# An attention and expert kernel on one core: second sequence's norm ahead of the split, key parts stored once

## The reference, cut to what matters

```python
x = x + _L0_xattn_ref(_layernorm(x), ctx, ...)          # stage A
h = _layernorm(_layernorm(x), ln_w, ln_b)               # norms u, b
hc = conv(h, 3 taps per channel, causal)
q, k, v = split(hc @ attn_w)                            # 16 heads of 8
q = q * cos + _rotate_half(q) * sin;  k likewise
scores = einsum(q, k) / sqrt(8), causal
y = softmax(scores) @ v @ proj_w
...                                                     # experts
x = x + _L1_xattn_ref(_layernorm(x), ctx, ...)          # stage C: k, v = ctx @ Wkv, 16 heads of 64
x = x + _L1_ffn_ref(_layernorm(x), ...)
```

## Time and profile before

| what | value |
|---|---|
| median of 3 runs (lowest, highest) | 342.58 us (340.04, 346.72) |
| the profiled execution's own time | 340.81 us |
| its span in the trace | 338.6 us |
| mean granted TensorE clock | 0.993 |
| PE, PE weight loads, DVE, ACT, POOL busy, share of the span | 93%, 65%, 72%, 65%, 38% |
| of the chain that ended last: PE, DVE, ACT, DMA | 58%, 16%, 14%, 3% |

### The profile page before, as it was taken

One profiled execution on the slowest core, in us unless ns is written; L12 is line 12 of the kernel. 1 busy time (PEld: TensorE's weight loads), 2 busy tenths in 40 slices (PEclk: granted clock), 3 DMA queues, 4 the chain that ended last, 5 costly groups with the idle time before them and its releaser, 6 DMA issues.

```text
span 338.6 us, 6802 instructions
## 1 busy us (share of the span) xinstructions
PE 315.3 (93%) x2270; PEld 220.6 (65%) x2270; DVE 245.2 (72%) x758; ACT 220.0 (65%) x649; POOL 128.1 (38%) x183
## 2 busy tenths in 40 slices
PE   8799989998989999999989998998999999999886
PEld 3348778665554433345446998985778687878675
DVE  4988875784898988888811552479788877887576
ACT  1488885375365756756676765754676667686995
POOL 3455564110641444410640440410685434535400
PEclk9999999999999999999998999999999999999999
DMA  7590000076763430091001003100100000000002
GB/s 213 196 274 10 2 0 2 8 243 170 209 206 89 113 102 3 1 326 52 5 31 56 2 31 111 33 1 2 54 20 15 0 2 1 3 0 0 2 0 65
DMA packets 21881, 22.47 MB, mean 66 GB/s; under 512 B 3894, under 2 KB 18646, under 8 KB 21846
## 3 DMA queue, kind: packets, MB, share of 16 engines
q1 hardware_dynamic: 18982, 16.78, 17.4%
q10 hardware_dynamic: 2352, 4.20, 3.7%
q0 software_dynamic: 512, 1.05, 1.0%
HBM read 14.22 MB, written 7.60 MB: 64 GB/s over the span
## 4 chain that ended last, share of the span: by engine, by line
PE 58%; DVE 16%; ACT 14%; issue 5%; POOL 4%; DMA 3%; SPq 0%; ACTq 0%; POOLq 0%
PE PS L1388 51%; PE PS L1442 5%; DVE PS L872 5%; ACT big L1167 5%; ACT big L1364 3%; POOL big L529 2%; DVE big L690 2%; DVE big L715 2%; DMA big<-in_A_WkT 2%; ACT big L1305 1%; ACT big L1141 1%; DMA XN<-scr_y,pos 1%; DVE XN L667 1%; ACT cw L1141 1%; PE PS L1704 1%
## 5 line engine op out<-in xcount | busy, mean ns | idle before, releaser
L1388 PE MATMUL PS<-big 128*128 128x128 f32 (+10 forms) x592 | 93.3, 308 | 7.0 <-DVE big L690 2.1
L1388 PEld LDWEIGHTS PS<-big 128*128 128x128 f32 (+3 forms) x592 | 56.2, 150 | 39.7 <-DVE mB L872 18.2
L529 POOL TENSOR_TENSOR big<-big,urec 128x1024 f32<-128x1024 f32 x24 | 45.6, 1900 | 60.2 <-DVE urec L722 45.4
L1167 ACT ACTIVATE big<-big 128x154 f32<-128x154 f32 x192 | 60.5, 319 | 10.6 <-DVE big L690 5.6
L872 DVE CUSTOM_DVE_ANT_0 PS<-PS,later 128x128 f32<-128x128 f32 (+3 forms) x128 | 60.1, 517 | 8.9 <-PE PS L1388 7.7
L1305 ACT ACTIVATE big<-PS 128x1024 f32<-128x1024 f32 (+3 forms) x64 | 43.2, 701 | 25.0 <-PE PS L1388 25.0
L1141 ACT ACTIVATE big<-PS 128x1280 f32<-128x1280 f32 (+2 forms) x30 | 32.3, 1088 | 27.0 <-PE PS L1442 24.5
L1388 PE MATMUL PS<-kkC,XT 128*128 128x462 f32 (+1 forms) x96 | 36.0, 511 | 1.9 <-DVE big L715 1.9
L1167 ACT ACTIVATION_READ_ACCUMULATOR big<-big 128x1 f32 x192 | 36.2, 189 | 0.0
L517 POOL TENSOR_TENSOR rstd<-ve,minus_half 128x4 f32<-128x4 f32 (+2 forms) x13 | 13.2, 1017 | 56.3 <-DVE ve L662 56.3
L1388 PEld LDWEIGHTS PS<-vwCm,big 128*128 128x128 f32 x256 | 30.8, 192 | 3.9 <-ACT big L1141 1.3
(11 more groups left out here) (192 smaller groups left out, 499.7 us busy)
## 6 DMA issues: line engine op xcount, KB each, us to landing
scr_qk<-big SPq DMA_DIRECT2D x12, 384.0 KB, 3.3
big<-scr_qk SPq DMA_DIRECT2D x16, 288.0 KB
big<-in_wv ACTq DMA_DIRECT2D x1, 2048.0 KB, 7.9
scr_x<-zrow SPq DMA_DIRECT2D x2, 448.0 KB, 6.9
scr_y<-big SPq DMA_DIRECT2D x2, 448.0 KB, 3.4
X<-in_x ACTq DMA_DIRECT2D x2, 256.0 KB, 3.3
big<-in_A_WoT ACTq DMA_DIRECT2D x1, 512.0 KB, 4.7
cw<-in_C_Wk SPq DMA_DIRECT2D x1, 512.0 KB, 5.2
```

What stands on the lines that cost most here:

```text
L529: pool.tensor_tensor(pn[:, 0:GH * P].rearrange("p (h k) -> p h k", h=GH), Pt[u % 3][:, :, 0:KM], r.to_broadcast([P, GH, KM]), ALU.mult).th ...
L1167: i = act.activation(Pt[u % 3][:, h, :], Pt[u % 3][:, h, :], ACT.Exp, accum_out=usum[:, u % 3, h:h + 1])
L1388: return pe.matmul(o, lhsT, rhs, start=start, stop=stop)
```

## The change

For sequence 1, the statistics and the application of norm b move on DVE ahead of `split_first`, with `add_rotated` between them. `weigh_router` moves from ring step 1 to in front of `rotate(1)`. The table numbers move: sequence 1 is transposed after job 16 instead of 25, its query and key matmuls and its `xv` come after job 24 instead of 29, jobs 28 to 49 instead of 32 to 49 stand among the maxima (two each at steps 5 and 13), and the first maxima are turned after job 40 instead of 44. `values(0)` on ACT comes after the first maxima's copy, and sequence 0's ones and zeros in `vaug` are written by two memsets on POOL. Key parts are stored once in `scr_k` (24 rows), and each group of `ks` is loaded by three transfers of 24 rows.

```diff
-        scr_qk = nc.dram_tensor("scr_qk", (B, 2, SPLIT, HB, T), BF16, kind="Internal").ap()
+        scr_q = nc.dram_tensor("scr_q", (B, SPLIT, HB, T), BF16, kind="Internal").ap()
+        scr_k = nc.dram_tensor("scr_k", (B, SPLIT // 3, HB, T), BF16, kind="Internal").ap()
...
-        F_QKV = (14,30)
-        F_LN = 26
-        F_LATE = 32
-        F_VALUES = 42
-        F_MAX = 45
+        F_QKV = (14, 25)
+        F_LN = 17
+        F_LATE = 26
+        F_FIRST = 28
+        F_VALUES = 38
+        F_MAX = 41
+        M_TWICE = (5, 13)
...
-                    sp.dma_start(scr_qk[b, 1].rearrange("(x y d) h t -> y (d h) x t", x=3, y=3)[a],
-                                 P3[:, 1, a, :].unsqueeze(1).to_broadcast([P, 3, T])).then_inc(scr_written[b], 16)
+                    sp.dma_start(scr_k[b].rearrange("(y d) h t -> y (d h) t", y=3)[a], P3[:, 1, a, :]).then_inc(scr_written[b], 16)
...
-                    sp.dma_start(ks[b][0:SPLIT, hs, :], scr_qk[b, 1, :, hs, :]).then_inc(stack_ready[b][g], 16)
-                    sp.dma_start(qs[b][0:SPLIT, hs, :], scr_qk[b, 0, :, hs, :]).then_inc(stack_ready[b][g], 16)
+                    for x in range(3):
+                        sp.dma_start(ks[b][SPLIT // 3 * x:SPLIT // 3 * (x + 1), hs, :], scr_k[b, :, hs, :]).then_inc(stack_ready[b][g], 16)
+                    sp.dma_start(qs[b][0:SPLIT, hs, :], scr_q[b, :, hs, :]).then_inc(stack_ready[b][g], 16)
...
             pool.wait_ge(part_ready[1], 3)
+            pool.wait_ge(preC_act, sum(j[2] for j in PREC[:F_VALUES]))
+            v = vaug[:, 0].rearrange("p t h m -> p (t h) m")
+            pool.memset(v[:, :, HDB:HDB + 1], 1.0).then_inc(v_ready, 1)
+            pool.memset(v[:, :, HDB + 1:32], 0.0).then_inc(v_ready, 1)
             split_maxima(1)
...
             rotate(0)
+            ln_b_stats(1)
             add_rotated()
+            ln_apply("b", U, XN, 1)
             split_first()
-            ln_b_stats(1)
-            ln_apply("b", U, XN, 1)
             convolve(1)
+            weigh_router()
             rotate(1)
...
-            copy_C(F_LN, F_VALUES)
+            copy_C(F_LN, F_MAX)
+            copy_maxima(0)
             act.wait_ge(preC_act, sum(j[2] for j in PREC[:F_VALUES]))
             values(0)
-            no_values(0)
-            copy_C(F_VALUES, F_MAX)
-            copy_maxima(0)
...
-            fold_C(F_QKV[1], F_LATE)
-            pe.wait_ge(preC_act, sum(j[2] for j in PREC[:F_LATE]))
-            pe.wait_ge(qkv_read, 4 * B)
+            fold_C(F_QKV[1], F_FIRST)
+            pe.wait_ge(preC_act, sum(j[2] for j in PREC[:F_LATE - 2]))
...
-            late = F_LATE
+            late = F_FIRST
             for m in range(M0):
                 scores_for_maximum(m)
-                if m >= 2 and late < len(PREC):
+                for _ in range(2 if m in M_TWICE else 1):
                     fold_C(late, late + 1)
                     late += 1
-                if late == F_MAX:
-                    turn_maxima(0)
+                    if late == F_MAX:
+                        turn_maxima(0)
```

More of the change, by code:

```diff
@@ L470, in _ @@
                     sp.wait_ge(part_ready[b], a + 1)
-                    sp.dma_start(scr_qk[b, 1].rearrange("(x y d) h t -> y (d h) x t", x=3, y=3)[a],
-                                 P3[:, 1, a, :].unsqueeze(1).to_broadcast([P, 3, T])).then_inc(scr_written[b], 16)
-                    sp.dma_start(scr_qk[b, 0].rearrange("(x y d) h t -> x (d h) y t", x=3, y=3)[a],
+                    sp.dma_start(scr_k[b].rearrange("(y d) h t -> y (d h) t", y=3)[a], P3[:, 1, a, :]).then_inc(scr_written[b], 16)
+                    sp.dma_start(scr_q[b].rearrange("(x y d) h t -> x (d h) y t", x=3, y=3)[a],
                                  P3[:, 0, a, :].unsqueeze(1).to_broadcast([P, 3, T])).then_inc(scr_written[b], 16)
@@ L816, in ln_b_stats, with weigh_router @@
                 ln_stats("b", U, b, lambda: dve.wait_ge(ln_norm["u"], QT * b + QT))
+            def weigh_router():
+                dve.wait_ge(ld_b, 64)
+                dve.wait_ge(ld_vec, 16)
+                dve.wait_ge(zeroed, Z_ALL)
+                dve.tensor_scalar(rw2[:], rw[:], vec[:, V_LN2W:V_LN2W + 1], None, ALU.mult).then_inc(rw2_ready, 1)
+                dve.tensor_scalar(ln2b[:], ones[:], vec[:, V_LN2B:V_LN2B + 1], None, ALU.mult).then_inc(rw2_ready, 1)
             def convolve(b):
@@ L916, in x_plus_u @@
                 own.wait()
[L919 to L925, removed]
             def centre_router():
@@ L1023, in _ @@
                     normalise_group(*divmod(g, 4))
-                if s == 1:
-                    weigh_router()
-                elif s == 3:
+                if s == 3:
                     centre_router()
@@ L1238, in values @@
                 copy(v[:, :, 0:HDB], XN[:, QT * b:QT * b + QT, :].rearrange("p t (h d) -> p (t h) d", h=HB)).then_inc(v_ready, 1)
-                copy(v[:, :, HDB:HDB + 1], ones[:, 0:QT * HB].unsqueeze(2)).then_inc(v_ready, 1)
             def no_values(b):
                 v = vaug[:, b].rearrange("p t h m -> p (t h) m")
+                copy(v[:, :, HDB:HDB + 1], ones[:, 0:QT * HB].unsqueeze(2)).then_inc(v_ready, 1)
                 copy(v[:, :, HDB + 1:32], ones[:, 0:32 - HDB - 1].unsqueeze(1).to_broadcast([P, QT * HB, 32 - HDB - 1]),
@@ L1534, in fold_C @@
                         pe.wait_ge(ln_T["b"], B)
-                        pe.wait_ge(qkv_read, 4 * B)
+                        pe.wait_ge(qkv_read, 4 * B - 2)
                     elif 3 <= n < F_LATE:
@@ L1640, in scores_for_maximum @@
                 if m % M_CHUNK == 0:
-                    pe.wait_ge(stack_ready[0][m // M_CHUNK], 32)
+                    pe.wait_ge(stack_ready[0][m // M_CHUNK], 64)
                 if m >= 3:
                     pe.wait_ge(s_max, m - 2)
+                elif m == 1:
+                    pe.wait_ge(qkv_read, 4 * B)
+                elif m == 2:
+                    pe.wait_ge(preC_act, sum(j[2] for j in PREC[:F_LATE]))
                 for j in range(2):
@@ L1654, in ring_scores @@
                 if n % M_CHUNK == 0:
-                    pe.wait_ge(stack_ready[b][n // M_CHUNK], 32)
+                    pe.wait_ge(stack_ready[b][n // M_CHUNK], 64)
                 if k < 2:
@@ L1662, in ring_scores @@
                 i.then_inc(s1_mm, 1)
-            late = F_LATE
+            late = F_FIRST
             for m in range(M0):
                 scores_for_maximum(m)
-                if m >= 2 and late < len(PREC):
+                for _ in range(2 if m in M_TWICE else 1):
                     fold_C(late, late + 1)
                     late += 1
-                if late == F_MAX:
-                    turn_maxima(0)
+                    if late == F_MAX:
+                        turn_maxima(0)
+            assert late == len(PREC)
             def outputs(s):
```

1 line of the change is left out of this document (removed).

## The result

The changed kernel is slower: 345.88 us median of four runs (343.68 to 347.82) against 341.31 for the kernel before in the same rounds (339.29 to 346.72). The ratio is 1.0127, 95% interval 1.0084 to 1.0170; on a second chip it was 1.0088 (1.0046 to 1.0129). The forecast of 337.5 and its range miss it. The profiled execution took 343.68 us (span 341.8, mean clock 0.989) against 340.81 before (0.993). It is the fastest of the four; the others, 345.55 to 347.82, had a mean clock of 0.980 to 0.983 and left no trace, so what follows explains this one execution, and where the others lost more is not shown.

What follows compares the result with a forecast made beforehand. PE was 93% busy, with PE and DVE near bounds together in the maxima. Gains of 3.5 us by the maxima's end and 0.3 in the ring, 3.8, took 340.81 to 337.0; it chose 337.5, range 334.5 to 341.5.

Steps and rivals of the forecast that it cites:

- Norm b ahead of the split: Sequence 1 before its scores: convolution ends 3.8 us earlier, at 78.4; PE ready for scores at 84.6 instead of 87.83.
- The stacks: Key stores and loads ahead of the first scores: group 0 lands at 84.5, scores start at 84.7, a gain of 3.1.
- rival 1: Ahead of the first scores: group 0 lands at 86 to 87, start gains 1.3, time 339.3; chance 0.15.
- A late store delays PE directly: Ahead of the first scores: the loads' five us of cover are gone, so a late store holds up PE.
- The maxima: Stretch from first scores to last maximum: 19.6 us instead of 19.97, ending at 104.3 against 107.8.
- Three steps in flight let PE put folds into DVE's time: In the maxima: from step 0 on, the reason for taking 19.6 us, nearer to DVE's time.
- rival 2: In the maxima: four added folds cost their full 2.3, PE bounds the stage at 21.5 us, time 339.4; chance 0.15.
- The hole of 1.15: DVE's wait at 102.47 in the maxima, behind ACT's values, ones and zeros: goes away, 1.0 us counted as gained.
- the fourfold price: POOL's memsets of ones and zeros: 1.35 us by columns, free up to four times that, since POOL idled 5.35 us.
- The router: At the ring's start: `weigh_router` moved from step 1 to in front of `rotate(1)` gains 0.3 of 0.6 us.
- The DMA rule: Stack loads: 72 rows and 24 rows both run on 12 of 16 engines, so the keys' rate does not change.
- Rivals 4 and 5: Slower by SP's queue of load issues, about 345.5, or by transfers in series, 342.5; chance 0.04 each.

Runs made afterwards that it cites:

- keys thrice: Old key stores (three copies) and 72-row loads put back into the changed kernel: ratio 1.0114 to the kernel before; put into `split_in_the_middle`: 0.9954.
- best_parts: The kernel before with key parts stored once and loaded in three, constants by POOL and values behind the first maxima's copy: ratio 0.9981.
- split_in_the_middle: Changed kernel with sequence 1's statistics and the sum, then split, then norm b applied; later query and key matmuls, two folds fewer in the maxima: 0.9918.
- packet earlier: Changed kernel with the 15 matmuls of 512 columns at PE's start cut into 60 of 128: ratio 1.0000 to the kernel before, 1.0010 on one chip.
- the clock held: Changed kernel with twelve unused matmuls of 512 columns on ones in PE's wait ahead of the first scores: ratio 1.0009 to the kernel before.

## Why the prediction was wrong, by its steps

- **Norm b ahead of the split: right in its result.** Convolution's end 78.68 (forecast 78.4), query matmuls 78.74 (78.8), PE ready 84.55 (84.6). The sum does not fill POOL's wait free of charge: the root took 1.85 instead of 1.01, and DVE waited 0.90.
- **The stacks: the step that failed first.** Forecast 84.5, measured 87.22. The terms: the last part's stores issued from 76.74 instead of 76.35 (0.39 late, with the slower root), the first load 4.76 us behind that instead of 3.15 (1.61 late, of which the packet's tail is 1.49, 4.39 against 2.90), and 5.7 us of loads instead of 5.0 (0.7). The upper end for the loads, 87, was named; I took the value near the lone group of the earlier trace rows, measured in a calm queue. Without the tail the loads took 6.7, so their length is not a constant of their size. In this case's numbers three transfers of 24 rows and one of 72 took 5.6 to 6.7; two of 72 took 5.5 in both kernels with keys thrice (81.60 to 87.07, 83.80 to 89.31). This is rival 1 (86 to 87, from a slow store), at 0.15, and a little more.
- **"A late store delays PE directly": true but not the whole price.** The prediction costed idle PE by its length. Waits of 1.83 us or more ahead of the first scores were followed by some 3.5 us at 1.2 GHz in the profiles of six kernels, with one exception (2.06, above), and none of 1.08 or less was. That costs 1.4 to 1.6 more (stretches of 22.75 to 22.86 us against 21.33 with 22 folds, 20.72 and 20.73 against 19.13 with 20).
- **The maxima: a term mis-sized.** Forecast 19.6, measured 21.33 at full clock. Its four folds more were put at 2.3 us of work, which DVE's time would nearly swallow; from 18 folds (18.76) to 22 they cost 2.57. "Three steps in flight let PE put folds into DVE's time" holds to 20 folds (19.13) and not for the last two. This is rival 2 (21.5), at 0.15. The hole of 1.15 went as forecast. POOL's memsets took 1.57 us (1.35 by the columns; the fourfold price did not come) and were hidden, and POOL still idled 4.16 us behind them.
- **The router: nothing gained.** From ring step 0 to step 4 it is 9.74 us before, 9.74 in `best_parts` with the router in step 1, and 9.73 in `split_in_the_middle` without it.
- **The DMA rule.** I wrote that the share of 0.81 agrees with 12 of 16 engines. Twelve of 16 could be busy 0.75 at most, and the changed kernel shows 0.82 from 85 to 86, with loads alone in flight (0.88 in the kernel with the packet earlier), and the 0.81 of the earlier trace rows was above 0.75 already. So the rows don't bear that reading out; that 24 rows keep the rate of 72 is roughly right (two loads of 72 rows 5.5 us, the four 5.6 to 6.7). Rivals 4 and 5 did not come: SP issues three loads in 1.13 to 1.56 us, and the four transfers don't take 9.2.

The sum at ring step 4: forecast 3.8 gained, measured 3.75 lost (120.27 against 116.52), a miss of 7.55. It is made up of 2.5 (start), 1.7 (folds), 1.5 (first fall), 1.55 (second fall: step 0 to 4 takes 11.29 instead of 9.74) and 0.3 (router). The second fall is not shown to come from the change, since what decides it is open. Without both falls the loss at step 4 would be some 0.7 us (3.75 less 1.53 and 1.55, an estimate), which goes with the ratio of 1.0009 with the clock held. Rivals 1 and 2 came true together, where the prediction only let one happen at a time, and the clock was not in it at all. The early arrival of PE was real. With the split ahead of norm b's application, and the table set so that PE has folds until the stacks land, the same ideas give 0.9918.

## What to carry to other kernels

When an edit lets the busiest engine arrive earlier, find what it will wait for there, and give it as much work as that wait lasts: here two folds on the wrong side of the wait cost 2.2 us in the maxima, and the wait that they would have filled 1.5 as clock. In this kernel a new wait of PE of some 2 us cost more than its length in six of the seven profiles above; price it so, and add the rivals' costs up, since late data and a fuller stage come from the same edit. Take a transfer's time from a row with the same traffic around it, not from the calmest one.

## What the hardware showed that I had not expected

- Granted clock: after waits of PE of 1.83, 2.10, 2.67, 2.99, 3.25 and 4.26 us it fell to the level of 1.2 GHz for about 3.5 us (for example 0.50 from 90 to 92 behind the wait of 3.25); a fall costs 1.4 to 1.6 us here. Behind 2.06, 1.08, 0.69, 0.52 and the wait filled with matmuls it did not fall. A further fall, at the ring's start, comes and goes between kernels with the same wait of 0.61 us.
- One packet of instructions, 0.02 MB and 1.3% of the 16 engines in 4.39 us (0.9 us of one engine), in the midst of a store lengthened it from 2.9 to 4.4 us (a store of the larger size from 4.4 to 5.84 and 5.87): the last 1.4 us passed at 9 to 28 GB/s, and the loads wait for the whole store. Fifteen matmuls cut into 60 at the program's start moved it 7 and 15 us ahead in the changed kernel's two profiles and 7 us with the split in the middle.
- POOL's 128 x 4 multiply took 1.85 us with DVE's sum of two SBUF operands beside it and 1.01 without.
